# Token contexts in 64x64 tiles, a mask made by GpSimd, negated k weights, and the first contexts ahead of the last q

## What is computed

```python
def _linear_attn(x, Wq, Wk, Wv, Wo, bo):
    scale = DH ** (-0.25)                        # 8 heads of DH = 8 features
    q = softmax(split(x @ Wq) * scale, axis=-1)  # over the 8 features of a head
    k = softmax(split(x @ Wk) * scale, axis=-2)  # over the 64 tokens of a batch
    v = split(x @ Wv)
    context = einsum('bhnd,bhne->bhde', k, v)    # 8x8 for each head
    out = einsum('bhnd,bhde->bhne', q, context)
    return out @ Wo + bo

for i in range(4):
    x = x + _linear_attn(layernorm(x), ...)
    x = x + (gelu(layernorm(x) @ W1[i] + b1[i]) @ W2[i] + b2[i])
```

## Time and profile before

| | |
|---|---|
| median of three runs | 791.68 us |
| the profiled execution | 787.36 us, span 785.6 us |
| PE busy | 637.4 us, 81% of the span, 11679 instructions |
| DVE busy | 558.0 us, 71% |
| ACT busy | 362.5 us, 46% |
| POOL busy | 60.5 us, 8% |

### The profile page before, as it was taken

One profiled execution on the slowest core, in us unless ns is written; L12 is line 12 of the kernel. 1 busy time (PEld: TensorE's weight loads), 2 busy tenths in 40 slices (PEclk: granted clock), 3 DMA queues, 4 the chain that ended last, 5 costly groups with the idle time before them and its releaser, 6 DMA issues. The chain is left out here.

```text
span 785.6 us, 25353 instructions
## 1 busy us (share of the span) xinstructions
PE 637.4 (81%) x11679; PEld 445.4 (57%) x11679; DVE 558.0 (71%) x874; ACT 362.5 (46%) x517; POOL 60.5 (8%) x106
## 2 busy tenths in 40 slices
PE   5989964766899936767999757888678899899997
PEld 3867751324777713337777513335427778788754
DVE  3568888994488879983688889978433876758453
ACT  0034559500144579000244567645133787766763
POOL 3100000002000000002000000020001221212200
PEclk9999997998799969996899979999797999899999
DMA  9200000006000000024000000040015000000001
GB/s 347 93 3 3 4 23 1 1 2 236 9 3 3 3 1 1 2 74 170 3 3 3 3 8 2 2 174 4 2 28 182 2 1 1 1 2 1 2 0 28
DMA packets 13922, 28.12 MB, mean 36 GB/s; under 512 B 5612, under 2 KB 6124, under 8 KB 13688
## 3 DMA queue, kind: packets, MB, share of 16 engines
q1 hardware_dynamic: 13528, 25.77, 9.3%
q10 hardware_dynamic: 288, 0.73, 0.3%
HBM read 25.44 MB, written 1.05 MB: 34 GB/s over the span
## 5 line engine op out<-in xcount | busy, mean ns | idle before, releaser
L461 ACT ACTIVATE V<-ps,wts 128x1024 f32<-128x1024 f32 x96 | 101.7, 1110 | 258.2 <-PE ps L926 258.2
L592 DVE BATCH_NORM_STATS2 stats<-V 128x6 f32<-128x512 f32 x192 | 117.7, 677 | 24.5 <-ACT V L461 24.5
L926 PE MATMUL ps<-tab,A 64*128 64x128 f32 x1536 | 104.3, 281 | 13.6 <-ACT V L461 7.8
L926 PEld LDWEIGHTS ps<-tab,A 64*128 64x128 f32 x1536 | 91.1, 187 | 37.4 <-issue 22.2
L534 DVE STREAM_TRANSPOSE A<-V 128x2048 f32<-128x2048 f32 x48 | 107.3, 2276 | 6.2 <-ACT V L440 6.2
L440 ACT ACTIVATE V<-V,small 128x2048 f32<-128x2048 f32 x48 | 96.1, 2083 | 3.8 <-DVE small L639 3.8
L801 PE MATMUL ps<-A,tab 128*128 128x384 f32 x192 | 70.0, 509 | 33.0 <-DVE A L541 33.0
L789 PE MATMUL ps<-A,tab 32*32 32x512 f32 x1536 | 60.9, 652 | 37.1 <-DVE A L534 37.1
L801 PEld LDWEIGHTS ps<-A,tab 128*128 128x128 f32 x192 | 35.1, 193 | 77.0 <-DVE A L541 61.2
L583 DVE STREAM_TRANSPOSE A<-ps 128x2048 f32<-128x2048 f32 (+1 forms) x27 | 55.6, 2072 | 24.9 <-PE ps L913 24.9
L541 DVE STREAM_TRANSPOSE A<-ps 128x1024 f32<-128x1024 f32 x48 | 56.5, 1217 | 11.5 <-PE ps L789 11.5
(11 more groups left out here) (256 smaller groups left out, 896.9 us busy)
## 6 DMA issues: line engine op xcount, KB each, us to landing
A<-in_modes SPq DMA_DIRECT2D x32, 384.0 KB, 7.4
r_ky<-in_modes SPq DMA_DIRECT2D x16, 384.0 KB, 5.8
wl<-in_layers SPq DMA_DIRECT2D x3, 452.0 KB, 4.8
V<-in_pixels SPq DMA_DIRECT2D x1, 1024.0 KB, 12.6
wm<-in_mixture SPq DMA_DIRECT2D x1, 874.5 KB, 6.3
tab<-in_table SPq DMA_DIRECT2D x1, 656.5 KB
A<-in_turned SPq DMA_DIRECT2D x1, 512.0 KB
tower_out<-A SPq DMA_DIRECT2D x4, 128.0 KB, 2.3
```

Of the source, the lines that this page charges most:

```text
L461: nc.scalar.activation(Vm[:, 2 * h:2 * h + 2, r, 512 * q:512 * (q + 1)], bank(half_of_u(q, r) + 2 * h, 2).rearrange("p (m n) -> p m n", m= ...
L592: last = nc.vector.bn_stats(stats[:, 16 * q + 4 * r + m, :], Vm[:, m, r, 512 * q:512 * (q + 1)])
L926: last = nc.tensor.matmul(ps[:, at:at + P], G[(2 * q + quad) % 4][rows, x:x + P], inv_y[rows, :], start=step < 2 and quad == 0, stop=step ...
```

## The change

Four things change in the attention half.

- A context matmul takes one feature half and one batch: 64 tokens, 64 columns of turned k, 64 columns of v, in a 64x64 tile of the array. There are 32 in a layer instead of 16. `cx` has half the size, and the application (now in 64x64 tiles too) has 32 matmuls instead of 16.
- GpSimd makes `mask`, the table `own` times the reciprocals of k's sums, for a whole group in one instruction, behind its four products of q. VectorE multiplies contexts and mask in one instruction per group.
- GpSimd multiplies k's weights by minus the scale ahead of the layer, so that TensorE makes k negated and scaled. VectorE takes a minimum, which is the bias as it stands, and L1495 goes. TensorE waits for the weights before each k matmul (`s_wk`).
- TensorE makes the contexts of group 0 before it turns q of group 3.

```diff
-    own = np.kron(np.eye(2 * HEADS), np.ones((DH, DH)))
+    own = np.tile(np.kron(np.eye(HEADS), np.ones((DH, DH))), (2, 2))
...
-        cx = sb("cx", [P, 2 * NX])
+        cx = sb("cx", [P, NX])
+        mask = sb("mask", [P, NX])
...
+            def scale_keys(l):
+
+                pool.wait_ge(s_wl[l], 16)
+                keys = wl[:, l, W_K:W_K + P]
+                nc.gpsimd.tensor_scalar(keys, keys, -SCALE, 0.0, ALU.mult, ALU.add).then_inc(s_wk, 1)
+
+            def own_over_sums(l, g):
+
+                pool.wait_ge(s_krec, l * G + g + 1)
+                if l:
+                    pool.wait_ge(s_cx, (l - 1) * G + g + 1)
+                each = [P, GT, EMB]
+                nc.gpsimd.tensor_tensor(part(mask, g).rearrange("p (i e) -> p i e", e=EMB),
+                                        own[:, 0:EMB].unsqueeze(1).broadcast_to(each),
+                                        kst[:, 2, GT * g:GT * (g + 1)].unsqueeze(2).broadcast_to(each), ALU.mult).then_inc(s_mask, 1)
+
+            scale_keys(0)
...
+                        for g in range(G):
+                            own_over_sums(l, g)
+                        if l + 1 < DEPTH:
+                            scale_keys(l + 1)
...
-                    act.wait_ge(s_kmax, l * G + g + 1)
+                    act.wait_ge(s_kmin, l * G + g + 1)
                     for i in range(GT):
                         last = nc.scalar.activation(part(ke, g)[:, S * i:S * (i + 1)], bank(g, 1, S * i, S), ACT.Exp,
-                                                    bias=kst[:, 3, GT * g + i:GT * g + i + 1], scale=SCALE)
+                                                    bias=kst[:, 0, GT * g + i:GT * g + i + 1], scale=-1.0)
...
-                    link(nc.vector.reduce_max(kmax, bank(g, 1).rearrange("p (i n) -> p i n", n=S), X_AXIS))
-                    nc.vector.tensor_scalar(kshift, kmax, -SCALE, None, ALU.mult).then_inc(s_kmax, 1)
+                    nc.vector.tensor_reduce(kmin, bank(g, 1).rearrange("p (i n) -> p i n", n=S), X_AXIS, ALU.min).then_inc(s_kmin, 1)
...
-                    dve.wait_ge(s_krec, l * G + g + 1)
-                    for t in range(GP):
-                        for b in range(2):
-                            i = GT * g + 2 * t + b
-                            last = nc.vector.scalar_tensor_tensor(out=cx[:, P * i:P * (i + 1)], in0=bank(g, b, P * t, P),
-                                                                  scalar=kst[:, 2, i:i + 1], in1=own, op0=ALU.mult, op1=ALU.mult)
-                    last.then_inc(s_cx, 1)
+                    dve.wait_ge(s_mask, l * G + g + 1)
+                    found = bank(g, 0, 0, 1024).rearrange("p (b n) -> p b n", b=2)[:, :, 0:GP * EMB]
+                    nc.vector.tensor_tensor(part(cx, g).rearrange("p (t b e) -> p t b e", b=2, e=EMB),
+                                            found.rearrange("p b (t e) -> p t b e", e=EMB),
+                                            part(mask, g).rearrange("p (t b e) -> p t b e", b=2, e=EMB), ALU.mult).then_inc(s_cx, 1)
...
+                    pe.wait_ge(s_wk, l + 1)
                     nc.tensor.matmul(bank(g, 1), w[:, W_K:W_K + P], h, start=True, stop=True)
...
-                for g in range(G):
+                def turn_queries(g):
                     pe.wait_ge(s_qn, l * G + g + 1)
                     for t in range(GP):
                         last = nc.tensor.transpose(bank(g, 0, GW + P * t, P), part(qs, g)[:, P * t:P * (t + 1)], ident)
                     last.then_inc(s_qtr, 1)
-                for g in range(G):
+
+                def contexts(g):
+
                     pe.wait_ge(s_kqT, l * G + g + 1)
                     pe.wait_ge(s_vs, l * G + g + 1)
                     for t in range(GP):
-                        for b in range(2):
-                            rows = slice(S * b, S * (b + 1))
-                            last = nc.tensor.matmul(bank(g, b, P * t, P), kqT[rows, g, 0, P * t:P * (t + 1)],
-                                                    part(vs, g)[rows, P * t:P * (t + 1)], start=True, stop=True,
-                                                    tile_position=(S * b, 0))
+                        for par in range(2):
+                            for b in range(2):
+                                rows, at = slice(S * b, S * (b + 1)), P * t + EMB * par
+                                last = nc.tensor.matmul(bank(g, b, EMB * t, EMB)[EMB * par:EMB * (par + 1), :],
+                                                        kqT[rows, g, 0, at:at + EMB], part(vs, g)[rows, at:at + EMB],
+                                                        start=True, stop=True, tile_position=(S * b, EMB * par))
                     last.then_inc(s_ctx, 1)
+
+
+                for g in range(G - 1):
+                    turn_queries(g)
+                contexts(0)
+                turn_queries(G - 1)
+                for g in range(1, G):
+                    contexts(g)
                 for g in range(G):
                     pe.wait_ge(s_cx, l * G + g + 1)
                     for i in range(GT):
-                        last = nc.tensor.matmul(bank(g, 0, S * i, S), part(cx, g, 2)[:, P * i:P * (i + 1)],
-                                                kqT[:, g, 1, S * i:S * (i + 1)], start=True, stop=True)
+                        for par in range(2):
+                            rows = slice(EMB * par, EMB * (par + 1))
+                            last = nc.tensor.matmul(bank(g, 0, S * i, S)[rows, :], part(cx, g)[rows, EMB * i:EMB * (i + 1)],
+                                                    kqT[rows, g, 1, S * i:S * (i + 1)], start=True, stop=True,
+                                                    tile_position=(EMB * par, EMB * par))
                     last.then_inc(s_out, 1)
                 nc.tensor.matmul(bank(3, 1, 0, 2), centre, w[:, W_BO:W_BO + 2], start=True, stop=True).then_inc(s_bcol, 1)
                 pe.wait_ge(s_wcen, 2 * l + 1)
```

More of the change, by code:

```diff
@@ L1196, in token_kernel @@
         s_kv = sem("s_kv")
-        s_kmax = sem("s_kmax")
+        s_kmin = sem("s_kmin")
+        s_wk = sem("s_wk")
+        s_mask = sem("s_mask")
         s_qs = sem("s_qs")
@@ L1487, in _ @@
                     dve.wait_ge(s_q, l * G + g + 1)
-                    hmax, kmax, kshift = hst[:, 0, GH * g:GH * (g + 1)], kst[:, 0, GT * g:GT * (g + 1)], kst[:, 3, GT * g:GT * (g + 1)]
+                    hmax, kmin = hst[:, 0, GH * g:GH * (g + 1)], kst[:, 0, GT * g:GT * (g + 1)]
                     q3 = bank(g, 0, GW).rearrange("p (h d) -> p h d", d=DH)
```

## The result

The changed kernel took 771.57 us (median of four runs, 768.39 to 773.50), the kernel before 790.52 us in the same comparison: a ratio of 0.976, with an interval of 0.972 to 0.979. A second comparison with the same two kernels gave 773.35 against 790.33 us, 0.978 (0.975 to 0.982). So the change is worth 17 to 19 us. One execution of all those reported here, of the variant with the mask on VectorE, was in a slower state (1180.05 us) and stands in no ratio.

What follows compares the result with a forecast made beforehand. VectorE's masking was taken to set the last 4 us of the attention half. Gains of 3.5 us in layer 0 and 2.9 in each of three others, 12.2 in all, took 791.68 to 779.5 us; range 775 to 786.5.

Steps and rivals of the forecast that it cites:

- What bounds the kernel, and what the new half takes: Attention half: VectorE's masking sets the last 4 us; the new half takes 13.3 us instead of 16.24.
- VectorE's start 0.2 us earlier: Dropping L1495 starts VectorE's q sums 0.19 us earlier per layer, 0.77 us in layer 0.
- Contexts near 16 ns a record: Contexts in 64x64 tiles: near 16 ns a record, 0.25 us a group instead of 0.50.
- the drain: Two added tiling-mode changes per layer: no price in the sum; at 0.17 us each, 0.7 us in all, 780.2 us.
- Applications 31 ns a record: Applying contexts in 64x64 tiles, two at a time: 31 ns a record, 0.50 us a group.
- Masks 0.66 us each: GpSimd's four masks behind its q products: 0.66 us each, 0.72 as upper end.
- cx 0.42 us: VectorE's masking, one instruction per group: 0.42 to 0.43 us each, four replacing 16 that took 4.21 us.
- taking the half-clock stretches as they are: Layers 2 and 3: 2.9 us gained each, with the places where TensorE gets half its clock left unchanged.
- Rival 1: Attention half: TensorE, with less work, loses up to 1.7 us to half clock; 7.7 us gained, 784.0 us; chance 0.17.
- The low end: 775 us: applications at 14.8 ns, two half-clock stretches over contexts gone (1.15 us each), 1 us for a quicker spread.
- Rivals 2 and 3: GpSimd and VectorE hold each other up, 786.3 us, chance 0.06; 64x64 tiles run one after another, 797.6 us, chance 0.06.
- rival 2: Each GpSimd mask waits for one VectorE instruction; 1.2 us gained per layer, 5.4 in all, 786.3 us; chance 0.06.

Runs made afterwards that it cites:

- turns first: The changed kernel with group 0's contexts behind all four turns of q, as before the change; 774.72 us, ratio 0.979 to the kernel before.
- the two late variants: The changed kernel with eight or four turns of the identity added ahead of layer 0's first variance; 774.69 us (ratio 0.981) and 772.28 us (0.978).
- The filler experiment on the kernel before: The kernel before with turns of the identity, overwritten right after, added in TensorE's waits ahead of q and k turns; 784.12 us, ratio 0.992.
- the masking per tile: The changed kernel with no mask and sixteen 128x64 scalar_tensor_tensor a layer; 780.36 us, ratio 0.987; with added turns in TensorE's waits 782.44 us, 0.989.

## Why the prediction was wrong, step by step

**What bounds the kernel, and what the new half takes: right.** At full clock a layer was to end its applications 13.3 us after its first q matmul and does so after 13.21. The distance of layers was to fall by 2.9 us and falls by 2.89. In layer 0, 3.5 us were forecast. From its first reduction of q (606.44; 608.51 after) to its bias matmul are 15.4 us before and 11.8 after, 3.6 us less. That is 3.6 + 3 x 2.9 = 12.3 us of gain at full clock, the forecast's sum of 12.2.

**Its terms.** VectorE's start 0.2 us earlier, in layer 0 0.8: measured 0.20 and 0.79. Contexts near 16 ns a record: about 17.5 (the weight loads of two groups, 32 in 0.56 us); the first group, between turns, takes 0.39 us in the chain for 16, where 0.25 was put, and the last 0.46. The first contexts follow the third turn in the chain with no gap (646.53 + 0.44 = 646.97), and the end came at 13.21 us; with two changes of tiling fewer (turns first) at 13.22. Little of the 0.14 us more for the first group reaches the end: the applications start 11.20 us after the first q matmul, and 11.13 with turns first. Of the drain for which the Trainium skill, "TensorEngine Tiling (Array Packing)", section Key Properties, led me to put 0.7 us beside the sum, nothing shows in the end. Applications 31 ns a record: 2.01 us for 64, 31.4. Masks 0.66 us each: one each 0.58, even faster. cx 0.42 us: 0.416. Two sub-steps were off, and harmless: the last two cx were to wait for their masks and don't, and group 1's cx was put at 650.57, where one instruction behind 650.23 is 650.65.

**The step that failed: "taking the half-clock stretches as they are".** The change in half-clock time was the term of the sum that was mis-sized: it was put at zero, and measured 3.6 to 5.0 us. The token stage fell from 194.2 and 195.6 us to 178.3 twice, by 15.9 and 17.3, of which 12.3 are the full-clock gain. In the sum of three layer distances the excess over full clock went from 3.8 and 5.5 us to 0 and 0 (1.6 and 1.6 in the two late variants); in layer 0 one more stretch of the second trace of before is gone; and against that stands the tail, where the changed kernel pays 1.6 us in both traces and the kernel before in one of two. So the traces give 15.9 to 17.3 us in all; the second comparison gave 17.0, and the 18.95 of the first has a lower bound of 16.6. The filler experiment on the kernel before shows from the other side that such a sum can be won without any of the change: 6.2 us.

**Rival 1 had the right subject and the wrong sign.** It said that less work for TensorE would mean more stretches in the new half, at up to 1.7 us each; the one that met contexts and applications, in the variants that start late, cost 1.0. I read it through the waits: in layer 1, TensorE does nothing but single turns between the third k turn and its contexts, for 3.0 us now (643.91 to 646.90 in the timeline) and 3.7 before (645.45 to 649.15). That the shorter wait is what made the difference is argued from the two traces; shown, by the fillers, is only that the waits of the kernel before brought on its stretches over contexts. The prediction had the evidence: it says itself that layers 2 and 3 already lose 1.15 us each, and layer 2's spreading 1.6. Such a term needed a forecast of its own, with a range on both sides, instead of a place among the rivals on one side only.

**The low end.** It allowed for two stretches over contexts gone (2.3 us) and a quicker spread of the runs (1 us) beside a cheaper application. The first was too little: it leaves out the stretches over spreadings (1.55 us each), and the first profile had caught the kernel before in a good execution, 787.36 us against a median of 790.3 of 19 timed runs, with one stretch over contexts less than the second.

**Rivals 2 and 3 did not occur.** GpSimd's products (631 ns) and masks (616 ns) kept their lengths beside VectorE; two diagonal tiles do run side by side, at 31.4 ns a record. What rival 2 feared does exist in another place: in the variant with the mask on VectorE, whose mask reads SBUF twice, GpSimd's scaling of weights took 468 ns in the three layers where it fell on a mask and 300 ns where it didn't, and that mask 468 ns, where the median is 426.

What stays open: how often each half is caught over many executions (six traces are few), what brings about the stretches over spreadings, why VectorE's first maskings pause in the kernel with negated k alone, and what is left between the 15.9 to 17.3 us of the traces and the 17 to 19 of the timed runs.

## What to carry to other kernels

Where the granted clock of TensorE falls within a stage, read it as a term of the sum: take the distance of two equal stages at full clock as the mechanism's measure, and the excess of the others as a price that a change can remove or bring back. Look past the end of the stage too: a stretch that is gone from the layers can stand behind them, as the one over the last spreading did. A change that shortens TensorE's waits can gain twice, and one that lengthens them can lose twice: the mask on VectorE cost 11.5 us, of which its waits for cx are 7.6. That the longer waits bring on the stretches of that variant is argued, not shown; for the masking per tile the fillers won nothing back. And half the clock costs what the engine that sets the pace loses by it: 1.55 us over a spreading, 1.0 to 1.2 over contexts and applications, and nothing over contexts that waited for VectorE.

## What the hardware showed that I had not expected

- Matmuls whose results are overwritten paid where TensorE waited anyway: ten of them ahead of the tokens made the start of the token stage 1.0 us shorter in the trace (5.94 to 4.95 us), and nine per layer in the kernel before (one ahead of each of the four q turns, 2 + 3 ahead of k turns) cut its time by 6.2 us.
- The same GpSimd instruction form took 629 to 631 ns with one broadcast input (the q products) and 616 ns with two (the masks), one each 0.58 us; a second broadcast input made it no slower. VectorE took 435 ns for the same mask (median 426), and 416 to 424 ns where one input lies in the accumulator memory.
- Matmuls in 64x64 tiles at all four positions run at 17.5 to 20 ns a record with 64 streamed columns (32 weight loads in 0.56 us; 64 records in 1.26), and two diagonal ones at 31.4 ns (64 records in 2.01 us).
- The same stretch at half clock had three prices in these traces: 1.55 us over a spreading, 1.15 over contexts of the kernel before, and none over contexts of the variant that masks per tile (32.30 us with it and without it).
